# Weighing all four heads of a graph-attention layer's edge messages on one engine instead of two

## The chip, the cores and the metric

The kernel runs on one core of one Trainium2 chip. The metric is the device time of one execution in microseconds (us); a lower time is better. A core has several engines that work side by side and wait for one another through semaphores: TensorE (PE, matmuls; PEld is its weight load), VectorE (DVE), ScalarE (ACT), GpSimd (POOL, which here also issues the gathers) and SyncE (SP, which issues plain transfers).

## The reference, cut to what matters

The program is four graph layers, one after the other, over 6250 nodes and 100000 edges. The change touches the first layer only, a graph attention with four heads of 64 columns:

```python
h = (x @ W).reshape(n, HEADS, C)                 # HEADS = 4, C = 64
e = a_src[src] + a_dst[dst]; e = jnp.where(e >= 0, e, NEG_SLOPE * e)
m = jax.ops.segment_max(e, dst, num_segments=n)
alpha = jnp.exp(e - m[dst])
denom = jax.ops.segment_sum(alpha, dst, num_segments=n)
alpha = alpha / (denom[dst] + 1e-16)
msg = alpha[:, :, None] * h[src]
out = jax.ops.segment_sum(msg, dst, num_segments=n)
```

The product `alpha * h[src]` is what is called weighing below: each gathered row of 256 values is multiplied, head by head, with four weights of its edge.

## The kernel before

The edges are sorted by destination and cut into 832 steps of 128 edges. Four steps are a group, 32 steps (eight groups) are a block, and there are 26 blocks. `gat_edges` (lines 580 to 919) runs them; `ends_apart` (line 95) writes the first and the last round out and loops over the others, two blocks to a round. The work of two blocks overlaps: in one turn, the logits, maxima and weights of block n are computed while block n-1 is weighed and summed, and block n+1 is gathered.

For one group the steps are these. GpSimd gathers four times 128 rows of 260 values from the node table into `e_rows` (line 664). The weights, `exp` of the logit less the maximum, are written once per block by ScalarE into PSUM (line 696) and once more beside the rows (line 698). Then the rows are weighed: VectorE takes heads 0 and 1 of the whole group in one operation (line 804, 128 partitions x 512 values), and ScalarE takes heads 2 and 3 in eight small ones (line 676, 128x64 each, one per step and head). VectorE counts up `weighed`, ScalarE `half_weighed`. TensorE waits for both (lines 722 and 723) and for the one-hot matrix of the group (line 924), and sums each step's rows by destination into one of four PSUM banks (line 727). VectorE adds each sum to the accumulator of its node tile (line 821).

The order of the work is written out by hand, engine by engine. For each group q of a turn VectorE weighs group q, adds the four sums of group q-1, and makes the one-hot matrix of group q+1; at q = 3 to 7 the work of the next block is put in between (logits at line 829, scans at lines 838 and 840, links at lines 846 to 853, tops at lines 860 to 868, arguments at line 900), and from q = 4 on two `spread` operations per q (line 788), whose data SyncE brings (line 650). GpSimd's gathers of group q of block n+1 go into the buffer of block n-1, so they wait until TensorE has summed group q of block n-1 (semaphore `summed`, lines 661 and 662). ScalarE's order in a turn is: weigh groups 0 to 3, copy the gather indices of block n+2 when block n has landed (line 691), weigh groups 4 and 5, `exp` for the rescale (line 694), weigh groups 6 and 7, and the two `exp` of the weights (lines 696 and 698). After the last turn the eight groups of the last block are weighed and summed with nothing beside them.

Of the kernel before, what the change touches and what calls it, by code (L numbers as in the profile page):

```python
# [18 lines left out]
ALU = mybir.AluOpType  # L19
ACT = mybir.ActivationFunctionType  # L20
AX = mybir.AxisListType

P = 128
N = 6250
E = 100000
D = 256
# [5 lines left out]
GROUP = 4  # L32
# [547 lines left out]
def gat_edges(nc, k):  # L580

    H = 4
    SB = P // H
    BLOCKS = STEPS // SB
    GB = SB // GROUP
    ROUNDS = BLOCKS // 2
# [4 lines left out]
    with ExitStack() as ctx:  # L591
        def sb(name, shape, dt=F32):
# [4 lines left out]
        idx = [sb(f"e0_idx{u}", [P, SB], I32) for u in range(2)]  # L597
        rows = [sb(f"e0_rows{u}", [P, SB, W]) for u in range(2)]
# [10 lines left out]
        step_down = sb("e0_step_down", [1, H])  # L609
        shrink = sb("e0_shrink", [1, H])  # L610
# [8 lines left out]
        drow_landed = [sem(f"e0_drow_landed{q}") for q in range(RING)]  # L619
        tables_landed = [sem(f"e0_tables_landed{u}") for u in range(2)]  # L620
        (spread_ready, looked_up, logit_ready, turned, local_ready, ends_ready, links_ready, step_ready, shrink_ready,
         back_ready, arg_ready, weight_ready, weighed, half_weighed, onehot_ready, summed, added, chain, cleared, half_cleared) = (
             sem(f"e0_{n}") for n in (
                 "spread_ready", "looked_up", "logit_ready", "turned", "local_ready", "ends_ready", "links_ready",
                 "step_ready", "shrink_ready", "back_ready", "arg_ready", "weight_ready", "weighed", "half_weighed", "onehot_ready",
                 "summed", "added", "chain", "cleared", "half_cleared"))
        block = ctx.enter_context(nc.Block())
        dloc_rows = k.rows_dloc.rearrange("(o s) l -> o (s l)", o=1)
# [39 lines left out]
        @block.scalar  # L668
        def _(act):
            for u in range(2):  # L670
                act.copy(idx[u][:], k.src_idx[:, u * SB:(u + 1) * SB]).then_inc(idx_ready, 1)
            def weigh(n, u, q):
                for s in range(q * GROUP, (q + 1) * GROUP):
                    for h in range(H // 2, H):
                        at = slice(h * (D // H), (h + 1) * (D // H))
                        ins = act.activation(rows[u][:, s, at], rows[u][:, s, at], ACT.Copy,  # L676
                                             scale=rows[u][:, s, D + h:D + h + 1])
                ins.then_inc(half_weighed, 1)

            for it in ends_apart(act, ROUNDS):  # L680
                for u in range(2):
                    n = it * 2 + u
                    start = isinstance(it, int) and it == 0 and u == 0
                    for q in range(GB):
                        if not start:
                            if q == 0:
                                act.wait_ge(weight_ready, 2 * n)
                            weigh(n - 1, 1 - u, q)
                        if q == 3 and not (isinstance(it, int) and it == ROUNDS - 1):
                            act.wait_ge(gathered[u], (it + 1) * (16 * SB))  # L690
                            act.copy(idx[u][:], k.src_idx[:, bass.ds((n + 2) * SB, SB)]).then_inc(idx_ready, 1)
                        if q == 5:
                            act.wait_ge(step_ready, n + 1)
                            act.activation(shrink[:], step_down[:], ACT.Exp).then_inc(shrink_ready, 1)
                    act.wait_ge(arg_ready, n + 1)
                    act.activation(k.psum[:, WEIGHT, 0:P], logit[:].rearrange("p h s -> p (h s)"), ACT.Exp
                                   ).then_inc(weight_ready, 1)
                    act.activation(by_step(rows[u][:, :, D:D + H]), logit[:], ACT.Exp).then_inc(weight_ready, 1)
            act.wait_ge(weight_ready, 2 * BLOCKS)
            for q in range(GB):  # L700
                weigh(BLOCKS - 1, 1, q)

        @block.tensor
        def _(pe):
            pe.sem_inc(summed, 2 * SB)
            pe.sem_inc(looked_up, 2)

            def look_up(n, q, js):
                g = n * GB + q
                pe.wait_ge(spread_ready, g + 1 + RING)  # L710
                for s in range(GROUP):
                    at = (q * GROUP + s) * 3 * H
                    ins = pe.matmul(k.psum[:, LOOK, at:at + 3 * H], spread[q % 2][:, s * P:(s + 1) * P],
                                    k.att16[:, bass.ds(js[q % 4 * GROUP + s], 1), :, :]
                                    .rearrange("p o h c -> p (o h c)"), start=True, stop=True)
                ins.then_inc(looked_up, 1)

            def block_steps(n, half):
                return load_indices(nc, pe, k.step_j, n * SB + half * 16, 16, NODE_TILES - 1)

            def add_up(n, u, q):
                pe.wait_ge(weighed, n * GB + q + 1)
                pe.wait_ge(half_weighed, n * GB + q + 1)
                pe.wait_ge(onehot_ready, n * GB + q + 1 + 1)
                for s in range(GROUP):
                    pe.wait_ge(added, n * NADD + q * GROUP + s + (3 if q else 1))
                    pe.matmul(k.psum[:, s, 0:W], onehot[q % 2][:, s, :], rows[u][:, q * GROUP + s, :],  # L727
                              start=True, stop=True).then_inc(summed, 1)

            for half in range(2):  # L730
                js = block_steps(0, half)
                for q in range(half * 4, half * 4 + 4):
                    look_up(0, q, js)
            for it in ends_apart(pe, ROUNDS):
                for u in range(2):
                    n = it * 2 + u
                    start = isinstance(it, int) and it == 0 and u == 0
                    end = isinstance(it, int) and it == ROUNDS - 1 and u == 1
                    for q in range(GB):
                        if not start:  # L740
                            add_up(n - 1, 1 - u, q)
                        if q == 3:
                            pe.wait_ge(logit_ready, n + 1)
                            pe.transpose(k.psum[:, TURN, 0:P], logit[:].rearrange("p h s -> p (h s)"), k.ident[:]
                                         ).then_inc(turned, 1)
                        if q == 4:
                            pe.wait_ge(local_ready, n + 1)
                            pe.matmul(k.psum[0:1, TURN, P:2 * P], local[:, P - 1:P], k.ident[:], start=True, stop=True)
                            pe.matmul(k.psum[0:1, TURN, 2 * P:3 * P], local[:, 0:1], k.anti[:], start=True, stop=True
                                      ).then_inc(ends_ready, 1)  # L750
                            pe.transpose(k.psum[:, BACK, 0:P], local[:], k.ident[:])
                        if q == 5:
                            pe.wait_ge(links_ready, n + 1)
                            pe.matmul(k.psum[:, BACK, P:3 * P], k.ones_row[:],
                                      links[:].rearrange("o a h s -> o (a h s)"), start=True, stop=True)
                            pe.wait_ge(shrink_ready, n + 1)
                            pe.matmul(k.psum[:, BACK, 3 * P:3 * P + H], k.ones_row[:], shrink[:], start=True, stop=True
                                      ).then_inc(back_ready, 1)
                        if q >= 4 and not end:
                            if q % 2 == 0:  # L760
                                js = block_steps(n + 1, (q - 4) // 2)
                            for ahead in (2 * (q - 4), 2 * (q - 4) + 1):
                                look_up(n + 1, ahead, js)
            for q in range(GB):
                add_up(BLOCKS - 1, 1, q)

        @block.vector
        def _(dve):
# [29 lines left out]
            def weigh(n, u, q):  # L798
                if q == 0:
                    dve.wait_ge(weight_ready, 2 * n + 2)  # L800
                at = slice(q * GROUP, (q + 1) * GROUP)
                w = k.psum[:, WEIGHT, 0:P].rearrange("p (h s) -> p s h", h=H)[:, at, 0:H // 2]
                half = rows[u][:, at, 0:D // 2].rearrange("p s (h c) -> p s h c", h=H // 2)
                dve.tensor_tensor(half, half, w.unsqueeze(3).to_broadcast([P, GROUP, H // 2, D // H]), ALU.mult
                                  ).then_inc(weighed, 1)

            def rescale(n, j):
# [2016 lines left out]
```

## Time and profile before

| | us |
|---|---|
| median of three runs | 6793.4 |
| lowest and highest | 6783.46 and 6804.74 |
| profiled execution | 6801.05 |
| span of the profiled execution, first to last instruction | 6799.1 |
| VectorE busy over the span | 4607.3 (68%) |
| ScalarE busy over the span | 2723.6 (40%) |
| GpSimd busy over the span | 4049.3 (60%) |
| TensorE busy over the span | 4665.7 (69%) |

All four layers share these totals, and the first layer's edges are one stage from about 250 to 1543 us. The views that are used are: the busy time of each engine in stretches of the span; the groups of instructions by line in a stretch; the timeline of one engine, in which each row has the start, the duration, the engine, the line, what is written from what, a count, and in brackets the idle time before it and what ended it; the view of one line, with its shortest, median and longest duration; and the list of waits. "issue" in brackets means that the profile shows nothing that the engine waited for. A DMA that is named as the releaser by a name of another stage (`n_x<-in_x`) stands for a semaphore that was used again: in this stage GpSimd's gathers wait for TensorE's sums and for the index copy alone.

### The profile page before, as it was taken

The page shows a single profiled execution, that of the slowest core. Times are in us where ns is not written, and L with a number is a line of the kernel's source. Part 1 is how long each engine was busy: PE and PEld are TensorE (multiplying, and loading weights), DVE is VectorE, ACT ScalarE, POOL GpSimd, SP SyncE. Part 2 cuts the span into 40 slices and gives each one's busy share as a digit, 9 for nine tenths or more (in the row PEclk, how much of TensorE's full clock was granted, in tenths as well). Part 3 has the DMA queues.
Part 4 walks back from the last instruction along what each step waited for, and adds up shares of the span by engine and source line. Part 5 has one row for each costly group of instructions (what it writes and reads, how often), then busy time and mean ns, then how long its engine had stood idle before and what let it go on. Part 6 is the DMA issues. An engine that isn't in the chain of part 4 may idle for free. (4 is left out here: it accounts for less than half of the span.)

```text
span 6799.1 us, 102254 instructions
## 1 busy us (share of the span) xinstructions
PE 4665.7 (69%) x18460; PEld 3459.3 (51%) x18461; DVE 4607.3 (68%) x11409; ACT 2723.6 (40%) x8089; POOL 4049.3 (60%) x3687
## 2 busy tenths in 40 slices
PE   7366666660566666787777777775577777777799
PEld 5233433340333343466666666664455555555688
DVE  4366666668445445577777777775589999999554
ACT  0133333345233333342111111112288998899543
POOL 1566666641666666525888888883367777777110
PEclk9576676775677767797777777777788888889899
DMA  6344444434555555414888888886556666666110
GB/s 205 105 108 108 108 109 109 109 78 134 170 176 180 178 176 178 138 65 94 136 135 135 134 135 135 135 129 186 179 163 185 188 189 190 183 189 186 37 32 28
DMA packets 697432, 941.29 MB, mean 138 GB/s; under 512 B 98671, under 2 KB 553935, under 8 KB 697264
## 3 DMA queue, kind: packets, MB, share of 16 engines
q0 software_dynamic: 270896, 581.23, 37.1%
q1 hardware_dynamic: 406928, 338.53, 17.2%
q10 hardware_dynamic: 19440, 19.79, 0.8%
q14 instruction: 124, 1.02, 0.0%
q8 instruction: 44, 0.72, 0.0%
HBM read 756.06 MB, written 183.11 MB: 138 GB/s over the span
## 5 line engine op out<-in xcount | busy, mean ns | idle before, releaser
L1810 POOL DMA_INDIRECT gcn<-c_update,c_target x784 | 1231.7, 1571 | 258.7 <-issue 208.9
L664 POOL DMA_INDIRECT e_rows<-hrow,e_idx x832 | 823.4, 990 | 466.5 <-issue 230.1
L2186 POOL DMA_INDIRECT s_rows<-kv,s_idx x832 | 797.6, 959 | 391.6 <-issue 222.9
L1202 POOL DMA_INDIRECT g_rows<-x,g_idx x784 | 776.5, 990 | 386.9 <-issue 226.9
L727 PE MATMUL psum<-e_rows,e_onehot 128*128 128x265 f32 x1664 | 637.5, 537 | 231.5 <-issue 97.7
L1321 PE MATMUL psum<-g_rows,g_onehot 128*128 x1664 | 614.9, 534 | 222.3 <-ACT g_rows L1225 174.0
L2300 PE MATMUL psum<-queries_sums,s_spread 128*128 x1664 | 540.6, 482 | 248.7 <-issue 123.5
L1283 DVE TENSOR_TENSOR acc<-acc,psum 128x1024 f32 x208 | 253.6, 1219 | 596.5 <-remote 352.4
L1321 PEld LDWEIGHTS psum<-g_rows,g_onehot 128*128 128x128 f32 x1664 | 423.4, 267 | 428.9 <-issue 352.6
L727 PEld LDWEIGHTS psum<-e_rows,e_onehot 128*128 128x128 f32 x1664 | 380.6, 253 | 428.9 <-issue 194.6
L1783 ACT COPY acc<-psum 128x512 f32<-128x512 f32 x208 | 121.8, 586 | 1183.1 <-PE psum L1742 758.7
L1765 PE MATMUL psum<-support,acc 128*128 x1664 | 586.7, 514 | 0.0
L1742 PE MATMUL psum<-acc 128*128 128x128 f32 x1664 | 324.1, 356 | 367.3 <-DVEq L1661 256.7
L2300 PEld LDWEIGHTS psum<-queries_sums,s_spread 128*128 128x128 f32 x1664 | 378.5, 238 | 375.8 <-issue 312.7
L2248 ACT ACTIVATE s_rows<-s_rows 128x32 f32<-128x32 f32 x2496 | 549.3, 306 | 1.7
L821 DVE TENSOR_TENSOR acc<-acc,psum 128x265 f32 x832 | 357.5, 430 | 280.0 <-issue 143.2
L1225 ACT ACTIVATE g_rows<-g_rows (+1 forms) x196 | 207.1, 1056 | 787.1 <-DVE g_rows L1276 644.9
L1742 PEld LDWEIGHTS psum<-acc 128*128 128x128 f32 x1664 | 290.3, 259 | 451.1 <-issue 307.1
L1765 PEld LDWEIGHTS psum<-support,acc 128*128 128x128 f32 x1664 | 413.9, 261 | 72.3 <-issue 0.3
L2315 PE MATMUL psum<-s_rows,s_onehot 128*128 128x264 f32 x1664 | 429.0, 403 | 9.0 <-ACT s_onehot L2240 5.8
L2468 DVE SCALAR_TENSOR_TENSOR queries_sums<-queries_sums,keep,psum 128x264 f32 x832 | 400.3, 481 | 41.8 <-issue 20.5
L676 ACT ACTIVATE e_rows<-e_rows 128x64 f32<-128x64 f32 x1664 | 406.9, 334 | 9.4 <-issue 8.4
(387 smaller groups left out, 9580.1 us busy)
## 6 DMA issues: line engine op xcount, KB each, us to landing
g_attr<-in_edge_attr SPq DMA_DIRECT2D x196, 512.0 KB
acc<-rows_src SPq DMA_DIRECT2D x208, 256.0 KB
e_drow<-rows_dloc SPq DMA_DIRECT2D x208, 128.0 KB
acc<-in_edge_feat SPq DMA_DIRECT2D x832, 32.0 KB
s_drow<-rows_dloc SPq DMA_DIRECT2D x208, 128.0 KB
n_sums<-gcn SPq DMA_DIRECT2D x100, 256.0 KB
e_rows<-hrow,e_idx POOLq DMA_INDIRECT x832
edge_rows<-c_edge_rows SPq DMA_DIRECT2D x208, 64.0 KB
```

The costliest lines, as they stand in the source:

```text
L664: pool.indirect_dma_start(rows[u][:, s, 0:D + H], None, k.hrow, bass.IndirectOffsetOnAxis(ap=idx[u][:, s:s + 1], axis=0)).then_inc(gathere ...
L676: ins = act.activation(rows[u][:, s, at], rows[u][:, s, at], ACT.Copy, scale=rows[u][:, s, D + h:D + h + 1])
L727: pe.matmul(k.psum[:, s, 0:W], onehot[q % 2][:, s, :], rows[u][:, q * GROUP + s, :], start=True, stop=True).then_inc(summed, 1)
L1202: pool.indirect_dma_start(rows[:, s, :], None, k.x1, bass.IndirectOffsetOnAxis(ap=idx[:, s:s + 1], axis=0)).then_inc(gathered[n % ROUND], 16)
L1321: pe.matmul(parts[:, bass.ds(to[st], 1), :].rearrange("p o d -> p (o d)"), onehot[q % 2][:, s, :], rows[:, bass.ds(m[st], 1), :].rearrange ...
L1742: ins = pe.matmul(k.psum[:, b, s * P:(s + 1) * P], onehot[b][:, s, :], same[b][:, s, :], start=True, stop=True)
L1765: ins = pe.matmul(k.psum[:, 2 + 2 * b + s // 2, (s % 2) * D:(s % 2 + 1) * D], mix[b][:, s * P:(s + 1) * P], k.support[:, bass.ds(j[q * GRO ...
L1810: pool.indirect_dma_start(k.gcn[a], bass.IndirectOffsetOnAxis(ap=target[:, at:at + 1], axis=0), update[:, at, :], None, compute_op=ALU.add ...
L2186: pool.indirect_dma_start(rows[at.u][:, st, 0:2 * D], None, k.kv, bass.IndirectOffsetOnAxis(ap=idx[at.u][:, st:st + 1], axis=0)).then_inc( ...
L2248: ins = act.activation(mine, mine, ACT.Copy, scale=rows[at.u][:, s, 2 * D + h:2 * D + h + 1])
L2300: ins = pe.matmul(k.psum[:, LOOK + s // 2, (s % 2) * D:(s % 2 + 1) * D], spread[at.b][:, s * P:(s + 1) * P], k.q[:, bass.ds(j[s], 1), :].r ...
L2315: pe.matmul(k.psum[:, s, 0:W], onehot[at.b][:, s, :], rows[at.u][:, at.q * GROUP + s, D:SLOT], start=True, stop=True).then_inc(summed, 1)
```

## The change

VectorE's weighing of a group goes from heads 0 and 1 to all four heads, still in one operation (128x512 becomes 128x1024, with the weights read from PSUM as before). ScalarE's weighing function, its eight calls per turn and the eight calls after the last turn are gone, as is the semaphore `half_weighed` with TensorE's wait for it. ScalarE's index copy and its `exp` for the rescale keep their order, without the weighings between them.

```diff
         def _(act):
-            def weigh(n, u, q):
-                for s in range(q * GROUP, (q + 1) * GROUP):
-                    for h in range(H // 2, H):
-                        at = slice(h * (D // H), (h + 1) * (D // H))
-                        ins = act.activation(rows[u][:, s, at], rows[u][:, s, at], ACT.Copy,
-                                             scale=rows[u][:, s, D + h:D + h + 1])
-                ins.then_inc(half_weighed, 1)
-
             for it in ends_apart(act, ROUNDS):
                 for u in range(2):
                     n = it * 2 + u
-                    start = isinstance(it, int) and it == 0 and u == 0
-                    for q in range(GB):
-                        if not start:
-                            if q == 0:
-                                act.wait_ge(weight_ready, 2 * n)
-                            weigh(n - 1, 1 - u, q)
-                        if q == 3 and not (isinstance(it, int) and it == ROUNDS - 1):
-                            act.wait_ge(gathered[u], (it + 1) * (16 * SB))
-                            act.copy(idx[u][:], k.src_idx[:, bass.ds((n + 2) * SB, SB)]).then_inc(idx_ready, 1)
-                        if q == 5:
-                            act.wait_ge(step_ready, n + 1)
-                            act.activation(shrink[:], step_down[:], ACT.Exp).then_inc(shrink_ready, 1)
+                    if not (isinstance(it, int) and it == ROUNDS - 1):
+                        act.wait_ge(gathered[u], (it + 1) * (16 * SB))
+                        act.copy(idx[u][:], k.src_idx[:, bass.ds((n + 2) * SB, SB)]).then_inc(idx_ready, 1)
+                    act.wait_ge(step_ready, n + 1)
+                    act.activation(shrink[:], step_down[:], ACT.Exp).then_inc(shrink_ready, 1)
...
-            act.wait_ge(weight_ready, 2 * BLOCKS)
-            for q in range(GB):
-                weigh(BLOCKS - 1, 1, q)
...
             def add_up(n, u, q):
                 pe.wait_ge(weighed, n * GB + q + 1)
-                pe.wait_ge(half_weighed, n * GB + q + 1)
                 pe.wait_ge(onehot_ready, n * GB + q + 1 + 1)
...
                 at = slice(q * GROUP, (q + 1) * GROUP)
-                w = k.psum[:, WEIGHT, 0:P].rearrange("p (h s) -> p s h", h=H)[:, at, 0:H // 2]
-                half = rows[u][:, at, 0:D // 2].rearrange("p s (h c) -> p s h c", h=H // 2)
-                dve.tensor_tensor(half, half, w.unsqueeze(3).to_broadcast([P, GROUP, H // 2, D // H]), ALU.mult
+                w = k.psum[:, WEIGHT, 0:P].rearrange("p (h s) -> p s h", h=H)[:, at, :]
+                part = rows[u][:, at, 0:D].rearrange("p s (h c) -> p s h c", h=H)
+                dve.tensor_tensor(part, part, w.unsqueeze(3).to_broadcast([P, GROUP, H, D // H]), ALU.mult
                                   ).then_inc(weighed, 1)
```

## Rows read from the trace of the kernel before

**Rows 1.** Busy time of each engine in a stretch of the stage (PE, PEld, DVE, ACT, POOL)
```profile
300.00:1400.00 1100.00, 702.73 (x2346) 430.37 (x2345) 698.91 (x1749) 362.73 (x1496) 704.28 (x711) 0.70 0.41 109
```

**Rows 2.** Groups of instructions by line, 300 to 1475 us: busy, mean, idle before
```profile
L664 POOL DMA_INDIRECT e_rows<-hrow,e_idx x758 | 752.2, 992 | 423.0 <-issue 207.1 <-DMA n_x<-in_x 144.2 <-PE psum L727 71.7
...
L804 DVE TENSOR_TENSOR e_rows<-e_rows,psum 128x512 f32<-128x512 f32 x188 | 127.9, 680 | 4.1 <-issue 4.1
```

**Rows 3.** Timeline of GpSimd: gathers at which a block's turn begins
```profile
392.92 1.27 POOL L664 DMA_INDIRECT e_rows<-hrow,e_idx  x1 [2.27 <-PE psum L727]
...
1337.98 1.28 POOL L664 DMA_INDIRECT e_rows<-hrow,e_idx  x1 [2.26 <-PE psum L727]
```

**Rows 4.** Timeline of GpSimd: one block's turn and the begin of the next
```profile
1139.44 1.28 POOL L664 DMA_INDIRECT e_rows<-hrow,e_idx  x1 [2.86 <-PE psum L727]
...
1164.11 0.96 POOL L664 DMA_INDIRECT e_rows<-hrow,e_idx  x1 [0.30 <-issue]
1168.86 0.95 POOL L664 DMA_INDIRECT e_rows<-hrow,e_idx  x1 [3.78 <-DMA n_x<-in_x]
...
1182.20 0.95 POOL L664 DMA_INDIRECT e_rows<-hrow,e_idx  x1 [2.89 <-DMA n_x<-in_x]
...
1188.71 1.27 POOL L664 DMA_INDIRECT e_rows<-hrow,e_idx  x1 [1.78 <-PE psum L727]
```

**Rows 5.** Timeline of VectorE: the weighing of group 5 and an add after it
```profile
1152.24 0.68 DVE L804 TENSOR_TENSOR e_rows<-e_rows,psum 128x512 f32<-128x512 f32 x1
...
1158.72 0.43 DVE L821 TENSOR_TENSOR acc<-acc,psum 128x265 f32 x1 [3.00 <-issue]
```

**Rows 6.** VectorE's register operations of line 818 from 1153 to 1168 us
```profile
L818 DVEq ALU_OP  x4: 16/696/702, 1153.0 to 1160.8; - x4
```

**Rows 7.** Those of line 819 from 1139 to 1151 us
```profile
L819 DVEq ALU_OP  x12: 40/40/40, 1139.5 to 1149.4; - x12
```

**Rows 8.** Timeline of VectorE: weighings of groups 6, 7 and 0, a wait between
```profile
1168.35 0.68 DVE L804 TENSOR_TENSOR e_rows<-e_rows,psum 128x512 f32<-128x512 f32 x1
...
1173.82 0.68 DVE L804 TENSOR_TENSOR e_rows<-e_rows,psum 128x512 f32<-128x512 f32 x1
...
1179.52 0.35 DVE L788 TENSOR_SCALAR e_spread<-e_drow,lane 128x512 bf16<-128x512 bf16 x1 [2.00 <-issue]
...
1183.28 0.68 DVE L804 TENSOR_TENSOR e_rows<-e_rows,psum 128x512 f32<-128x512 f32 x1
```

**Rows 9.** Page, costliest groups: a VectorE operation of 1024 values with PSUM input
```profile
L1283 DVE TENSOR_TENSOR acc<-acc,psum 128x1024 f32 x208 | 253.6, 1219 | 596.5 <-remote 352.4
```

**Rows 10.** Timeline of ScalarE: weighings of groups 0 to 3, a wait of the next turn
```profile
1128.14 7.75 ACT L676 ACTIVATE e_rows<-e_rows 128x64 f32<-128x64 f32 x32
...
1166.64 0.20 ACT L694 ACTIVATE e_shrink<-e_step_down 1x4 f32<-1x4 f32 x1 [24.10 <-issue]
```

**Rows 11.** Timeline of VectorE: the weighing of group 0 in that turn
```profile
1133.81 0.69 DVE L804 TENSOR_TENSOR e_rows<-e_rows,psum 128x512 f32<-128x512 f32 x1 [0.42 <-issue]
```

**Rows 12.** List of waits, 300 to 1500 us: waiter, releaser, us, times, longest
```profile
PE psum L727 <- ACT e_rows L676: 23.8, 11, 4.7
```

**Rows 13.** TensorE's wait for `half_weighed`, 300 to 1475 us: shortest, median, longest ns
```profile
L723 PEldq EVENT_SEMAPHORE  x176: 6/51/51, 334.9 to 1420.8; - x176
```

**Rows 14.** Timeline of TensorE: the eight matmuls that sum group 4
```profile
1148.63 3.12 PE L727 MATMUL psum<-e_rows,e_onehot 128*128 128x265 f32 x8 [0.61 <-DVE acc L821]
```

**Rows 15.** Timeline of VectorE: two weighings of the last block
```profile
1533.30 0.68 DVE L804 TENSOR_TENSOR e_rows<-e_rows,psum 128x512 f32<-128x512 f32 x1
...
1536.77 0.68 DVE L804 TENSOR_TENSOR e_rows<-e_rows,psum 128x512 f32<-128x512 f32 x1
```

**Rows 16.** Timeline of GpSimd: another block's turn, with one more wait in it
```profile
1238.55 1.27 POOL L664 DMA_INDIRECT e_rows<-hrow,e_idx  x1 [2.27 <-PE psum L727]
...
1274.07 0.95 POOL L664 DMA_INDIRECT e_rows<-hrow,e_idx  x1 [1.02 <-issue]
...
1287.97 1.40 POOL L664 DMA_INDIRECT e_rows<-hrow,e_idx  x1 [1.77 <-PE psum L727]
```

More of the change, by code:

```diff
@@ L621, in gat_edges @@
         (spread_ready, looked_up, logit_ready, turned, local_ready, ends_ready, links_ready, step_ready, shrink_ready,
-         back_ready, arg_ready, weight_ready, weighed, half_weighed, onehot_ready, summed, added, chain, cleared, half_cleared) = (
+         back_ready, arg_ready, weight_ready, weighed, onehot_ready, summed, added, chain, cleared, half_cleared) = (
              sem(f"e0_{n}") for n in (
                  "spread_ready", "looked_up", "logit_ready", "turned", "local_ready", "ends_ready", "links_ready",
-                 "step_ready", "shrink_ready", "back_ready", "arg_ready", "weight_ready", "weighed", "half_weighed", "onehot_ready",
+                 "step_ready", "shrink_ready", "back_ready", "arg_ready", "weight_ready", "weighed", "onehot_ready",
                  "summed", "added", "chain", "cleared", "half_cleared"))
```

## Prediction, made before the changed kernel was run

> **What bounds the kernel now.** I read the busy time by stretch first. Between 300 and 1400 us VectorE is busy 699 of 1100 us, GpSimd 704, TensorE 703 and ScalarE 363 [rows 1]: no engine is full, so the stage turns in a ring of waits, and what counts is which waits close it. The groups by line say who waits longest: the gathers, 758 of them, have 423 us of idle time before them, of which 207 us are the usual 0.30 us from one to the next and 216 us (144.2 + 71.7) end with TensorE's sums [rows 2].
>
> The timeline of GpSimd then gives the beat. The turns of 19 blocks lie between 392.92 and 1337.98 us, which makes 49.7 us for a block [rows 3]. In the turn that I take as the pattern, GpSimd begins at 1139.44 us, issues 20 gathers without a break (groups 0 to 4), ends the last at 1165.1, waits 3.78 us for the sum of group 5, issues eight, waits 2.89 us for group 7, issues four, and waits 1.78 us for group 0 of the next block, which it starts at 1188.71 [rows 4]. A gather takes 0.95 us and 0.30 to the next, so 32 of them need about 40.5 us of the 49.3; the rest is waiting.
>
> VectorE's timeline shows why the sums are late. Up to group 5 its operations follow one another without a gap, but after the weighing of group 5 at 1152.24 idle time that ends in "issue" lies before each add, 3.00 us of it before the one at 1158.72 [rows 5]. Its register operations, 40 ns each between 1139 and 1151 us [rows 7], take up to 702 ns between 1153 and 1168 [rows 6]. Such a slow stretch shows in nearly every turn, as I read the timelines. It begins 12 to 15 us after GpSimd has begun its 20 gathers and ends 2 to 3 us after it has stopped (1165.1 to about 1167.8), and a shorter one lies behind the next eight gathers (2.00 us of idle time before 1179.52 [rows 8]). What makes the register operations slow I can't read from the trace, only that it goes with a long unbroken run of gathers.
>
> So a turn has two parts. From 1139.4 to about 1167.8 GpSimd sets the time: VectorE's slow stretch ends when the gathers do, whatever VectorE had to do before it. From 1167.8 to 1188.7, some 21 us, VectorE sets it: it weighs groups 6 (1168.35), 7 (1173.82) and 0 of the next block (1183.28) [rows 8], TensorE sums group 0, and that sum starts GpSimd again.
>
> **The change, part by part.** *Longer weighings.* One of 128x512 takes 680 ns [rows 2]. An addition of 1024 values with one input in PSUM, of the same engine and type, takes 1219 ns [rows 9], and I take it for the new one, since only the number of values differs. That is +0.54 us each, 208 times: +112 us of VectorE's busy time. The bounds are 0.54 us and, if the narrow pattern (64 values per weight) cost per head, twice 680 = 1360 ns, or +0.68 us; I take 0.54.
>
> *Where they lie.* There are 24 turns in which a next block is gathered. In each, the weighings of groups 1 to 5 fall in the part that GpSimd sets; I cost them at nothing, and the cover is the wait for the end of 20 gathers. The sums of groups 1 to 4 stay ahead of the gathers: VectorE needs about 3.3 us for a group (3.47 in the last block [rows 15]), 3.9 after the change, GpSimd 5.0. If that cover is gone, they cost up to 5 x 0.54 = 2.7 us a turn. The weighings of groups 6, 7 and 0 are on the path: 3 x 0.54 = 1.6 us a turn.
>
> *The end.* In the last turn and in the last block after it nothing is gathered, and VectorE goes without a gap, 3.47 us from one weighing to the next [rows 15]. All 16 weighings are on the path there: 16 x 0.54 = 8.6 us.
>
> *ScalarE.* Its 1664 small weighings go. One run of 32 takes 7.75 us [rows 10], so a group takes 1.94 us, over 400 us of work in all. Was any of it on the path? At 1166.64 ScalarE has waited 24.10 us for VectorE's step [rows 10], and it weighs groups 0 to 3 from 1128.14 on, while VectorE comes to them only at 1133.81 [rows 11]. TensorE's waits put down to it are 23.8 us in 11 cases [rows 12], against 158 groups; in those that I looked at, VectorE's weighing ended later than ScalarE's, so I count no gain. If all of it were real, it would be -24 us. The index copy keeps its place, as it waits for the landing of the gathers and not for the weighings; the two `exp` come when VectorE's argument does. The cover that hid ScalarE's weighings is not used by anything else.
>
> *TensorE.* One wait per group goes, 51 ns each [rows 13]. Three groups a turn lie on the path, and 16 at the end: 24 x 3 x 0.05 = 3.6 us and 0.8 us less.
>
> **A rule to weigh.** Gathers beside VectorE's work take 0.95 us mostly, 1.27 to 1.40 us now and then [rows 4, 16], and the mean is 0.99 [rows 2]; nothing in the rows ties the long ones to the weighings. The Trainium skill, in "SBUF — State Buffer", section "SBUF: two separate sides", says that VectorE and GpSimd contend for one pair of ports, which an operation holds to its end, if VectorE runs in a two-port mode or reads two inputs from SBUF. The weighing reads one input from SBUF and one from PSUM, so by that rule it doesn't stop a gather at any length, and the sum stays as it is. Were it otherwise, GpSimd's own part would grow by as much as 8 x 0.54 us a turn, which is the same price as the first rival's.
>
> **The sum.** 24 x 1.6 + 8.6 - 3.6 - 0.8 = 38.9 + 8.6 - 4.4 = 43 us, with 24 x 1.62 = 38.9. The profiled execution had 6801.05 us (its span is 6799.1, the median of the three runs 6793.4, 7.7 us lower); on it the sum gives 6844 us, on the median 6793.4 + 43 = 6836.5 us. The prediction is of the median. About 0.3% (20 us) is what a measurement can tell from no change.
>
> **The rivals.** *Everything is on the path.* If the slow stretch begins at a place in VectorE's program and not at a time after GpSimd's start, it moves back with VectorE and its length stays: then all eight weighings count, 24 x 8 x 0.49 + 7.8 = 102 us, or 6895 us. For it speaks that the stretch begins near group 5 in most turns; against it, that it ends with GpSimd's stop in nearly all.
>
> *A leftover.* Between the forecast and this one: VectorE comes to the slow stretch 1.6 to 2.1 us later, does less in it, and takes up to 2 us of work along to the other side of it. That gives 43 + 48 = 91 us at the most, 6884 us. I count it to the forecast's own range.
>
> *The gathers hide it.* The eight gathers that follow have their own slow stretch, in which VectorE waits 2.00 us before 1179.52 [rows 8], and it ends with them. It can hide weighings 6 and 7. In the turn from 1238.55 to 1287.97 GpSimd waited once more, 1.02 us at 1274.07 [rows 16], and yet that turn took 49.4 us, less than the mean of 49.7. Then only the weighing of group 0 counts: 24 x 0.49 + 7.8 = 20 us, 6813 us; if that is hidden too, 8 us, 6801 us.
>
> *Faster.* The 20 gathers run through because the sum of group 4 is out (its matmuls run from 1148.63 to 1151.75 [rows 14]) just as the slow stretch begins (about 1152 [rows 5]). With VectorE some 2 us later it may come too late. Then GpSimd stops after 16 gathers, 5.0 us earlier, the slow stretch ends 5.0 us earlier, and GpSimd pays with one more wait of about 3.4 us. That is 1.6 us a turn gained, as VectorE and not GpSimd sets the rest: 43 us becomes -24 x 1.6 + 7.8 = -31 us, 6763 us. It decides when the slow stretch begins before group 4 is summed. Against it: a wait more has made no turn clearly shorter.
>
> *It doesn't do what it says.* If the operation took 1360 ns or more, the forecast's sum would be 24 x 3 x 0.68 + 16 x 0.68 - 4.4 = 55 us, 6849 us, or with everything on the path 6928 us.
>
> **How the numbers follow.** Forecast, with its leftover, 0.45 (its own range 6815 to 6884); everything on the path 0.20; the gathers hide it 0.20; faster 0.12; a dearer operation 0.03. The range runs from 6785 to 6908: it takes in the first three, and leaves out the faster case and the dearest one. Of the signs: slower by over 0.3% is the forecast, the first rival, the dearer operation and a quarter of the hidden case, 0.67 with what the forecast may lose; within 0.3% is most of the hidden case and the edges of the forecast and of the faster one, 0.23; faster 0.10.
>
> **What would show it.** Right: line 804 with 1024 values at about 1.22 us; the turns, read as the distance of gathers that end a wait for group 0, at about 51.2 us; 20 gathers in the first run; the weighings of groups 6, 7 and 0 further apart by 0.54 us each; the last block's weighings 4.0 us apart. Wrong: a turn of 53 to 54 us (everything counts), of 49.7 (hidden), or shorter with a first run of 16 gathers (faster). If the register operations are no longer slow, or slow for longer, my reading of the slow stretch as bound to the gathers is what fails.

## The result, and the profile after

The changed kernel takes 6831.5 us (median of six runs, 6820.1 to 6838.5), the kernel before 6792.8 us beside it (six runs): the ratio is 1.0054, with a 95% interval from 1.0041 to 1.0067. That is 37 to 39 us slower; 43 us were forecast. The profiled execution, the slowest of its six, has 6838.5 us against 6801.05, and a span of 6836.6 us. In it the stage's last sum ends 42.7 us later than before (1583.2 against 1540.5 us).

The new operation, in the view of its line (shortest, median and longest duration in ns, then who waited for it in us and times), and below it the gathers and the weighings in the groups by line from 300 to 1475 us, which answer to [rows 2]:

```profile
L785 DVE TENSOR_TENSOR e_rows<-e_rows,psum x208: 1195/1214/1222, 287.5 to 1578.9; 128x1024 f32<-128x1024 f32 x104
...
  PE psum L708: 84.6, 48
```

```profile
L664 POOL DMA_INDIRECT e_rows<-hrow,e_idx x735 | 716.5, 975 | 458.6 <-issue 220.9 <-PE psum L708 177.9 <-remote 59.8
...
L785 DVE TENSOR_TENSOR e_rows<-e_rows,psum 128x1024 f32<-128x1024 f32 x184 | 223.2, 1213 | 14.9 <-issue 14.8
```

It takes 1213 ns instead of 680, so +0.53 us. Over 20 turns the busy time by engine (PE, PEld, DVE, ACT, POOL) is, for before and then for after:

```profile
392.00:1386.00 994.00, 634.90 (x2123) 388.18 (x2121) 630.14 (x1579) 329.62 (x1360) 635.27 (x640) 0.70 0.41 109
```

```profile
394.00:1419.00 1025.00, 654.35 (x2122) 394.62 (x2121) 715.68 (x1580) 21.34 (x81) 623.53 (x640) 0.67 0.40 105
```

VectorE is busy 85.5 us longer in 20 turns (4.3 us a turn), and the 20 turns are 31 us longer (1.6 us a turn). The other 54.5 us came out of VectorE's idle time, which fell from 363.9 to 309.3 us. ScalarE's 308 us of work in them are gone. The granted clock of TensorE (the number before the last two) is 0.67 instead of 0.70.

The beat, from GpSimd's timeline, beside [rows 3]: the turns of 20 blocks lie between these two gathers, 51.25 us each (before, over the same 20 blocks, from 392.92 to 1386.58: 49.68).

```profile
394.44 1.27 POOL L664 DMA_INDIRECT e_rows<-hrow,e_idx  x1 [1.99 <-PE psum L708]
...
1419.42 0.95 POOL L664 DMA_INDIRECT e_rows<-hrow,e_idx  x1 [2.90 <-issue]
```

The turns are no longer alike. Of the 20, ten begin with 20 gathers in a run, as all of the same 20 did before, and last 52.2 us on average; the other ten begin with 16 and last 50.3 us. (Outside these 20, the trace of before has two such turns as well, of 51.2 and 46.6 us.) One of each, the gathers that end a wait (beside [rows 4]); where the profile names no engine of this core as the releaser it writes `remote`:

```profile
446.62 1.27 POOL L664 DMA_INDIRECT e_rows<-hrow,e_idx  x1 [3.00 <-PE psum L708]
478.40 0.95 POOL L664 DMA_INDIRECT e_rows<-hrow,e_idx  x1 [6.56 <-PE psum L708]
485.23 0.95 POOL L664 DMA_INDIRECT e_rows<-hrow,e_idx  x1 [1.63 <-PE psum L708]
490.38 0.95 POOL L664 DMA_INDIRECT e_rows<-hrow,e_idx  x1 [0.44 <-issue]
498.81 0.95 POOL L664 DMA_INDIRECT e_rows<-hrow,e_idx  x1 [3.20 <-PE psum L708]
```

```profile
596.88 0.95 POOL L664 DMA_INDIRECT e_rows<-hrow,e_idx  x1 [2.47 <-PE psum L708]
620.32 0.95 POOL L664 DMA_INDIRECT e_rows<-hrow,e_idx  x1 [3.31 <-remote]
632.59 0.95 POOL L664 DMA_INDIRECT e_rows<-hrow,e_idx  x1 [2.52 <-remote]
647.25 0.95 POOL L664 DMA_INDIRECT e_rows<-hrow,e_idx  x1 [4.88 <-PE psum L708]
```

In the first of them GpSimd waits 6.56 us after 20 gathers, where before it waited 3.78 [rows 4]. These are two different waits, and TensorE's timeline tells them apart. Here are the last matmuls of group 5's sum before (1162.00), of group 5's sum in the first turn (475.45), and all those of group 4's sum in the second turn (608.87):

```profile
1162.00 1.25 PE L727 MATMUL psum<-e_rows,e_onehot 128*128 128x265 f32 x2 [1.54 <-issue]
```

```profile
475.45 2.14 PE L708 MATMUL psum<-e_rows,e_onehot 128*128 128x265 f32 x4 [1.55 <-DVE acc L802]
```

```profile
608.87 2.44 PE L708 MATMUL psum<-e_rows,e_onehot 128*128 128x265 f32 x8 [1.15 <-DVE e_rows L785]
```

A gather that waits for a sum starts 0.8 us after the sum's last matmul. The first turn shows it: the sum ends at 477.59 and the gather starts at 478.40. Before, the sum of group 5 ended at 1163.25, ahead of the end of the twentieth gather (1165.07), and the next gather still started only at 1168.86, 5.6 us after it. So the 3.78 us of [rows 4] aren't the wait for the sum of group 5, as the prediction reads them. They end just after VectorE's slow stretch does (about 1167.8). It is so in all 20 turns of before: the wait is 3.3 to 3.9 us long, whether the sum ended 2.1 or 11.8 us before the gather starts, and in 17 turns the sum was out before GpSimd stopped.

The turns that begin with 16 gathers in the changed kernel have the same wait (sum out at 611.31, gather at 620.32; 2.6 to 9.3 us after the sum in all ten). In its ten turns with 20 gathers the gather starts 0.81 or 0.82 us after the sum: there the sum itself is late. What holds GpSimd in the other case no record shows.

VectorE's timeline of the first turn shows why the sum of group 5 is late, and what became of the late weighings (beside [rows 5] and [rows 8]):

```profile
461.91 1.21 DVE L785 TENSOR_TENSOR e_rows<-e_rows,psum 128x1024 f32<-128x1024 f32 x1
467.97 0.43 DVE L802 TENSOR_TENSOR acc<-acc,psum 128x265 f32 x1 [4.85 <-issue]
472.16 0.43 DVE L802 TENSOR_TENSOR acc<-acc,psum 128x265 f32 x1 [3.77 <-issue]
...
478.91 1.21 DVE L785 TENSOR_TENSOR e_rows<-e_rows,psum 128x1024 f32<-128x1024 f32 x1
...
484.91 1.21 DVE L785 TENSOR_TENSOR e_rows<-e_rows,psum 128x1024 f32<-128x1024 f32 x1
...
492.65 1.22 DVE L785 TENSOR_TENSOR e_rows<-e_rows,psum 128x1024 f32<-128x1024 f32 x1 [0.33 <-issue]
```

Group 5 is weighed 15.3 us after the turn's begin (12.8 before) and group 6 at 32.3 us (28.9 before). From there to the next turn's begin it is 19.9 us, against 20.4 before. In the mean of 20 turns it is 29.05 us before and 30.61 after from the begin to the weighing of group 6, and 20.63 and 20.63 from there to the next begin: all of the growth lies in the part that I had called covered. But this is the mean of two kinds of turns. The ten with 20 gathers have 32.10 and 20.12 us, the ten with 16 have 29.13 and 21.15.

In the end it is 4.00 us from one weighing of the last block to the next, where [rows 15] have 3.47. From the stage's last gather to its last sum it is 65.3 us, against 58.1 before, so the end costs 7.2 us where 8.6 were reckoned:

```profile
1566.93 1.21 DVE L785 TENSOR_TENSOR e_rows<-e_rows,psum 128x1024 f32<-128x1024 f32 x1
1570.93 1.21 DVE L785 TENSOR_TENSOR e_rows<-e_rows,psum 128x1024 f32<-128x1024 f32 x1
```

### The profile page after: what moved, and what is told of

It is laid out like the page before. It is cut to its first block and busy times, and to the rows that moved or that the text cites. A ratio compares the mean times of both kernels' runs of the same rounds, so it can differ in the third digit from the quotient of the medians.

```text
span 6836.6 us, 100360 instructions
## 1 busy us (share of the span) xinstructions
PE 4685.1 (69%) x18460; PEld 3458.6 (51%) x18461; DVE 4725.0 (69%) x11409; ACT 2321.3 (34%) x6425; POOL 4037.1 (59%) x3687
## 5 line engine op out<-in xcount | busy, mean ns | idle before, releaser
L708 PE MATMUL psum<-e_rows,e_onehot 128*128 128x265 f32 x1664 | 670.7, 558 | 337.1 <-issue 128.5
L1302 PE MATMUL psum<-g_rows,g_onehot 128*128 x1664 | 629.8, 544 | 210.7 <-ACT g_rows L1206 172.4
L1264 DVE TENSOR_TENSOR acc<-acc,psum 128x1024 f32 x208 | 253.6, 1219 | 598.0 <-remote 327.8
L1682 DVE SCALAR_TENSOR_TENSOR c_update<-c_update,acc,psum 128x256 f32 x832 | 399.9, 481 | 12.2
```

What stands on the lines that cost most here:

```text
L1302: pe.matmul(parts[:, bass.ds(to[st], 1), :].rearrange("p o d -> p (o d)"), onehot[q % 2][:, s, :], rows[:, bass.ds(m[st], 1), :].rearrange ...
```

## Experiments

Three theories were held against each other: (1) the prediction's, by which the gathers cover the weighings of groups 1 to 5 and groups 6, 7 and 0 are paid; (2) every weighing is paid; (3) the early ones are paid in part, at the slow stretch. The runs met two conditions, which the time of the kernel before, taken beside each of them, tells apart: 6800.5 and 6804.4 us in the one, like the first measurement, and 6333.6 and 6333.2 us in the other. I call them the 6800 us and the 6333 us condition; the expectations below speak of chips with and without slow stretches. That the chip makes the difference isn't shown: the record numbers the chips, and has number 12 for the first group of runs at 6800 us, number 5 for one at 6333 us, and number 3 for one of each. Every ratio is against before in the same group of runs.

### Without gathers

Edit, in both kernels: from block 2 on nothing is gathered, and the waits for landed rows are met by a plain count. The first layer's sums are others, so only the time is read.

```diff
+                        if isinstance(it, int) and it == 0:
...
+                        else:
+                            pool.sem_inc(skipped[u], 1)
```

> The kernel before, with the gathers of blocks 2 to 25 left out (rows of the first two blocks are weighed again and again, so the first layer's sums are others). What is left is the pace of VectorE and TensorE alone. Theory 1: the slow stretches come with the gathers, so no register operation of VectorE takes 0.7 us, and a turn is VectorE's busy time of 31.6 us plus short waits, 33 to 36 us, the stage 330 to 400 us shorter where there were slow stretches. Rival (the slow stretches are VectorE's own, code or registers): they stay, and a turn is 45 us or more on a chip that shows them.

> The changed kernel with the same gathers left out. Theory 1 (without gathers VectorE alone sets the turn, so every weighing counts): 8 x 0.54 = 4.3 us more per turn than the kernel before without gathers, less up to 0.4 us for TensorE's wait; 24 x 4.0 = +96 us and +8 us at the end. Rival (TensorE or ScalarE sets the turn there, and the weighings are hidden): under 2 us more per turn.

Measured, one execution each, in the 6800 us condition (before 6800.5 us): 6488.1 us for before without gathers, 6577.4 us for after without them, so 89 us apart. The logits of two blocks that are 20 turns apart, from VectorE's timeline of each, give a turn of 36.34 and of 39.99 us:

```profile
410.33 0.55 DVE L840 TENSOR_REDUCE e_logit<-psum 128x128 f32<-128x384 f32 x1
...
1137.11 0.55 DVE L840 TENSOR_REDUCE e_logit<-psum 128x128 f32<-128x384 f32 x1
```

```profile
423.16 0.55 DVE L821 TENSOR_REDUCE e_logit<-psum 128x128 f32<-128x384 f32 x1
...
1223.03 0.55 DVE L821 TENSOR_REDUCE e_logit<-psum 128x128 f32<-128x384 f32 x1
```

The register operations before an add (the wait for a sum), shortest, median and longest in ns; the kernel before as it is, then before without gathers:

```profile
L819 DVEq ALU_OP  x704: 5/40/710, 338.3 to 1426.1; - x176
```

```profile
L830 DVEq ALU_OP  x704: 40/40/40, 327.8 to 1123.9; - x176
```

What follows: with the gathers out, VectorE is busy 622 of 727 us in 20 turns before and 706 of 800 after, and 3.65 of the 4.3 us of added work are paid in a turn. With them in, only 1.6 are. So the gathers do hide work of VectorE. And the slow register operations need the gathers: not one of the 704 takes over 40 ns without them, in either kernel, while the changed kernel with gathers had up to 1142 ns in the same group of runs. The sizes were expected a little otherwise: before without gathers became 312 us shorter, not 330 to 400, and 89 us lie between the two where 104 were expected.

### ScalarE's work gone, VectorE's as before

Edit: the changed kernel, but VectorE weighs heads 0 and 1 alone.

```diff
-                w = k.psum[:, WEIGHT, 0:P].rearrange("p (h s) -> p s h", h=H)[:, at, :]
-                part = rows[u][:, at, 0:D].rearrange("p s (h c) -> p s h c", h=H)
+                w = k.psum[:, WEIGHT, 0:P].rearrange("p (h s) -> p s h", h=H)[:, at, 0:H // 2]
+                half = rows[u][:, at, 0:D // 2].rearrange("p s (h c) -> p s h c", h=H // 2)
```

> ScalarE's weighings and TensorE's wait for them are gone, and VectorE weighs heads 0 and 1 alone as before; heads 2 and 3 stay unweighed, so the kernel leaves that part of the computation out. Theory 1 (ScalarE is never on the path): -4 us against before from TensorE's wait alone, turns at 49.6 us, which can't be told from no change. Rival (TensorE's 23.8 us of waits that the profile puts down to ScalarE are real, or ScalarE's work slows others): -24 us or more, turns at 48.7 us.

Measured: 6333.5 us against 6333.6, ratio 1.0001 (0.9992 to 1.0010), in the 6333 us condition. ScalarE's 1664 weighings weren't on the path there. But GpSimd's gathers follow one another without a break in that condition, so hardly anything that is taken from ScalarE could show. In the 6800 us condition, in which the prediction had costed ScalarE, it wasn't run alone.

### The weighings split by group

Edit for the early ones (groups 1 to 5 on VectorE alone, 0, 6 and 7 shared as before); for the late ones the two sets change places (the first lines are VectorE's, the next TensorE's, the last ScalarE's):

```diff
+                heads = H // 2 if q in (0, 6, 7) else H
-                w = k.psum[:, WEIGHT, 0:P].rearrange("p (h s) -> p s h", h=H)[:, at, 0:H // 2]
+                w = k.psum[:, WEIGHT, 0:P].rearrange("p (h s) -> p s h", h=H)[:, at, 0:heads]
...
+                if q in (0, 6, 7):
+                    pe.wait_ge(half_weighed, n * 3 + (0, 6, 7).index(q) + 1)
...
+                            if q in (0, 6, 7):
+                                weigh(n - 1, 1 - u, q)
```

> VectorE weighs all four heads for groups 1 to 5 of each block, ScalarE keeps heads 2 and 3 of groups 0, 6 and 7 alone. Theory 1 (GpSimd's 20 gathers cover the early groups): the turns stay at 49.7 us, only the 10 wide groups of the end cost, 10 x 0.49 = +5 us against before. Theory 2 (every weighing of VectorE counts): 24 x 5 x 0.49 + 5 = +64 us, turns at 52.2 us. Theory 3 (VectorE comes later to the slow stretch and carries up to 2 us of work over it in turns that still have 20 gathers in a run): +20 to +50 us.

> The complement: VectorE weighs all four heads for groups 0, 6 and 7, ScalarE keeps heads 2 and 3 of groups 1 to 5. Theory 1 (the late groups are the ones on the path): 24 x 3 x 0.49 + 6 x 0.49 = +38 us against before, turns at 51.2 us, nearly the whole of the change's cost. Theory 2 (every weighing counts): the same +38 us, but then the early half costs +64 us and the two don't add up to the change's +38 us. Theory 3 (the later slow stretch hides groups 6 and 7): +12 to +15 us, turns at 50.2 us.

Measured, in the 6333 us condition: early 1.0000 (0.9991 to 1.0010), late 0.9989 (0.9980 to 0.9998). None of the theories was tried by it: there were no slow stretches, and GpSimd gathered without a break. So both were run again:

> Groups 1 to 5 wide on VectorE, groups 0, 6 and 7 shared as before; once more, for a chip with slow stretches. Theory 1 (the gathers cover the early groups): +5 us against before, turns at 49.7 us, first runs of 20 gathers. Theory 3 (VectorE comes to the slow stretch some 2 us later; where the sum of group 4 then comes too late the first run ends at 16 gathers and the turn is 2 us shorter than one with 20): first runs mixed, turns at 49.7 to 51 us, 0 to +30 us. Theory 2 (all count): +64 us. On a chip without slow stretches, all give what was measured there, 0 to +5 us.

> Groups 0, 6 and 7 wide on VectorE, groups 1 to 5 shared as before; once more, for a chip with slow stretches. Theory 1: +38 us against before, turns at 51.2 us, first runs of 20 gathers, since the sum of group 4 is no later than before. If instead the eight gathers' slow stretch hides groups 6 and 7: +12 to +15 us, turns at 50.2 us. If the early groups make the change's cost, this kernel is at 0 to +10 us. On a chip without slow stretches: -9 to +5 us.

Measured: again in the 6333 us condition, early 1.0002 (0.9993 to 1.0011), late 0.9987 (0.9978 to 0.9996). The early ones alone were run a third time:

> Groups 1 to 5 wide, 0, 6 and 7 shared, for the third time, as both runs so far fell on a chip without slow stretches (there: 0 to +3 us). On a chip with them: theory 1 as predicted before the change was run (the 20 gathers cover groups 1 to 5, the cost is in groups 6, 7 and 0) gives +5 us, turns at 49.7 us, 29.0 us from the first gather of a turn to the weighing of group 6. The theory that the changed kernel's trace suggests (the part before group 6 grew from 29.0 to 30.6 us, the part after it stayed at 20.6 us, so the early groups make the cost) gives +30 to +42 us, turns at 51 us, first runs of 16 and of 20 gathers, 30.6 us up to the weighing of group 6.

Measured, in the 6800 us condition: 6819.7 us against 6804.4, ratio 1.0025 (1.0015 to 1.0035), +15 to +17 us. The turn is 50.02 us over 20 turns:

```profile
394.13 0.95 POOL L664 DMA_INDIRECT e_rows<-hrow,e_idx  x1 [2.70 <-DMA n_x<-in_x]
...
1394.51 1.28 POOL L664 DMA_INDIRECT e_rows<-hrow,e_idx  x1 [0.78 <-issue]
```

Fifteen of the 20 turns begin with a run of 16 gathers and last 49.1 us, four with 20 and last 53.2 us, one with four. Up to the weighing of group 6 it is 29.7 us, after it 20.3. Both numbers that were expected are missed: theory 1's +5 us is too little, the +30 to +42 us of the theory formed from the changed kernel's trace too much. The medians put the early groups at something under half of the cost, with their share of the end (10 x 0.53 = 5 us) in it; the rest, 14 to 23 us, is by subtraction the late groups'. That the two parts simply add up isn't shown, as the late groups weren't run alone in this condition. The turns themselves don't bear the subtraction out: those with 16 gathers last 49.1 us here and 50.3 in the changed kernel's first trace (49.9 in its second, below), those with 20 last 53.2 us here and 52.2 (51.8) there.

### The changed kernel again

> The changed kernel once more, beside before on the chip that this call gets. In the four runs so far before took 6333.6 us and not 6793, the turns were 41.0 to 41.4 us, all 32 gathers stood in one unbroken run and no register operation of VectorE was slow. If the chip is again such a one: theory (GpSimd's 32 gathers alone set the turn, 32 x 1.29 = 41.2 us, and VectorE has some 5 us a turn to spare) gives only the end, +8 us against before. If it is one with slow stretches: +37 to +43 us as first measured, turns at 51.2 us. Rival (VectorE's 0.54 us count on every chip): +100 us on either.

Measured, in the 6800 us condition: 6830.9 us against 6800.5, ratio 1.0054 (1.0038 to 1.0069). The ratio of the first result is there again. The profiled execution is the fastest of its six, 6818.9 us. Its turn is 50.25 us, with 14 of 20 turns beginning with 16 gathers and four with 20, and the stage's last sum ends 22.9 us later than in the trace of before, where it was 42.7 us in the first trace. So the mix changes from one execution to the next, and with it the length of the stage.

> The changed kernel on the same chip as the three above, as their measure. On a chip with slow stretches: +37 us against before, turns between 50.2 and 51.3 us with first runs of 16 and of 20 gathers. On a chip without them: theory (GpSimd's gathers alone set the turn) gives the end alone, +8 us; rival (VectorE's work counts) +100 us.

Measured, in the 6333 us condition: 6328.0 us against 6333.2, ratio 0.9987 (0.9978 to 0.9996). It is not slower there at all, by the interval even faster by a trifle, where +8 us were expected. The turn is 41.09 us, no gather of it waits longer than the usual 0.3 us, and no register operation is slow:

```profile
353.58 0.96 POOL L664 DMA_INDIRECT e_rows<-hrow,e_idx  x1 [0.30 <-issue]
...
1175.33 0.95 POOL L664 DMA_INDIRECT e_rows<-hrow,e_idx  x1 [0.31 <-issue]
```

```profile
L800 DVEq ALU_OP  x704: 40/40/40, 303.7 to 1202.3; - x176
```

GpSimd's 32 gathers at 1.28 us are the turn. VectorE's turn of 40 us, as it was without gathers, fits into it with 1 us to spare.

### The late groups wholly on ScalarE

Edit: ScalarE weighs all four heads of groups 0, 6 and 7 as soon as the weights are there, VectorE all four of groups 1 to 5 (first lines ScalarE's, last ones VectorE's).

```diff
+                        for q in (0, 6, 7):
+                            weigh(n - 1, 1 - u, q)
...
+                if q in (0, 6, 7):
+                    return
```

> ScalarE weighs all four heads of groups 0, 6 and 7 (48 small operations a block, right after the weights are there), VectorE all four heads of groups 1 to 5. Theory 1 (late groups on the path, early groups covered): VectorE's 0.60 us falls away three times a turn, 24 x 3 x 0.60 = -43 us, and at the end 6 x 0.60 gained and 10 x 0.54 lost, +2 us: -41 us against before, turns at 47.9 us. Theory 2 (every weighing of VectorE counts alike): -43 + 24 x 5 x 0.54 + 2 = +24 us. Theory 3 (early groups cost about 2 us a turn through the slow stretch): about +5 us.

> ScalarE weighs groups 0, 6 and 7 whole, VectorE groups 1 to 5 whole; once more, for a chip with slow stretches. Theory 1: 24 x 3 x 0.60 = -43 us in the turns and +2 us at the end, -41 us against before, turns at 47.9 us. If the early groups' 0.54 us are paid at the slow stretch: -10 to +5 us. On a chip without slow stretches: -11 us as measured there.

Measured, both times in the 6333 us condition: 0.9985 (0.9976 to 0.9994) and 0.9983 (0.9974 to 0.9992), some 11 us faster than before. It beats before there, and can't be told from the changed kernel (0.9987). In the 6800 us condition, where it was meant to gain 41 us, it wasn't run, and whether it is faster there stays open.

## Why the prediction was right, and where it wasn't

**The price of one weighing** was right: 1213 ns where 1219 were taken, +0.53 us, no dearer for its narrow pattern.

**The end** was right within 1.4 us: 4.00 us between weighings, and 7.2 us from the last gather to the last sum where 16 x 0.54 = 8.6 us were reckoned. **TensorE's shorter wait**, 4.4 us in the sum, is shown by no run: where ScalarE's work and this wait alone were taken out, 4 us less were expected and none measured, in the 6333 us condition.

**ScalarE costed at nothing** was tried only in the 6333 us condition, with 1.0001 when its work alone was taken out. Whether the 23.8 us of waits that the profile puts down to it [rows 12] are real in the 6800 us condition stays open (and the groups that they are set against are 188 by the count of [rows 2], not 158).

**"The gathers cover groups 1 to 5"** is the step that failed, in the turns with 20 gathers. The wait for the end of the 20 gathers did cover VectorE's lateness before, since the sum of group 5 had slack: in the turn of [rows 4] it ended 23.8 us after the begin and its gather started at 29.4. The prediction took GpSimd's stop for a wait for this sum, so it did not see the slack, nor how much of it there was. In the changed kernel's turn VectorE comes to the weighing of group 5 2.5 us later and has the four adds behind it (those of group 4's sums) in the slow stretch, with 4.85 us of idle time before the first. TensorE needs these adds for the sum of group 5, and that now ends 31.0 us after the begin, 7.2 us later. Of these, 4.8 us were slack and 2.4 us are paid. In all ten turns with 20 gathers the sum ends at 29.4 to 31.0 us, against 17.7 to 27.4 before, and they last 52.2 us on average, against 49.7. This is the leftover to which the prediction gave the range only.

**"Groups 6, 7 and 0 are paid"** was wrong in its balance. Group 6 to 7 did take 0.53 us more (5.47 before, 6.00 after; 0.44 us in the mean of 20 turns), and so did the stretch from group 0 to the next begin (0.49 us in the mean). But from group 7 to group 0 it was 9.46 us and is 7.74 in the turn shown, 9.25 and 8.31 in the mean: VectorE's waits for the `spread` rows and its idle time in the second slow stretch shrank. Line 788 had 111.2 us of idle time before its operations from 300 us to the end of the gathers, and its answer in the changed kernel (300 to 1510 us) has 28.2. By the timelines of the 20 turns, 1.6 us a turn of this drop lie between groups 7 and 0, and the larger part, 2.4 us net, ahead of the weighing of group 6:

```profile
L788 DVE TENSOR_SCALAR e_spread<-e_drow,lane 128x512 bf16<-128x512 bf16 x190 | 63.3, 364 | 111.2 <-DMA rows_src<-acc 73.0 <-issue 28.2 <-PE psum L713 6.4
```

```profile
L769 DVE TENSOR_SCALAR e_spread<-e_drow,lane 128x512 bf16<-128x512 bf16 x190 | 63.1, 368 | 28.2 <-DMA rows_src<-acc 16.8 <-issue 7.6 <-PE psum L695 1.1
```

That is akin to the rival "the gathers hide it", at work in the later part of the turn.

**The rival "faster"** is there too, with the sign that it named and without its gain. In half of the turns the first run ended at 16 gathers. The sum of group 4 ended 14.3 to 20.8 us after the begin in these, 13.2 to 14.8 in the other half and 11.6 to 14.3 before, which fits the rival's condition that the sum comes after the slow stretch has begun. But GpSimd's stop isn't the plain wait for it: in 7 of the 10 the sum was out before the sixteenth gather had ended. These turns are 1.9 us shorter than those with 20 (50.3 against 52.2 us) and still 0.6 us longer than before, where the rival had them 1.6 us shorter than before.

**The size was luck in part.** Two kinds of turns, +2.5 and +0.6 us, mixed to a mean of 1.57 us, which happens to lie at the forecast's 1.6. In the second trace of the changed kernel the same code gave +0.57 us a turn. The place was wrong, and the early-groups experiment shows it: +15 to +17 us where the forecast's steps give +5.

**A rival that nobody tried** is TensorE's clock. From 300 us to the end of the gathers the matmuls of the sums take 542 ns in the mean before and 565 after, at a granted clock of 0.70 and 0.67 over the 20 turns (0.69 in the second trace of the changed kernel). That is 0.2 us for the eight matmuls of a sum; how much of the 1.57 us it makes isn't shown.

**The rule that was weighed** held: with a VectorE operation nearly twice as long the gathers did not get longer, their mean went from 992 ns [rows 2] to 975. That agrees with the rule of the Trainium skill's "SBUF — State Buffer", section "SBUF: two separate sides".

**Everything on the path** fell: without gathers 3.65 us a turn are paid, with them 1.6. (The 6928 us that the prediction gives it with the dearer operation don't come out of its terms, which make about 6924; nothing hangs on it.)

**The slow stretch as bound to the gathers** held, but it is half of what it takes: the gathers, and the 6800 us condition. What that condition is stays open.

## What to carry to other kernels

When two engines pace each other in turns, ask of a covered stretch not only what ends it but what else has to be ready at that moment, and how long it has been ready. Compare the end of the work that is waited for with the end of the wait: here a gather that really waited for a sum started 0.8 us after it, and one that started 5.6 us after it waited for something else. The difference is slack, and the work moved into the cover used it up and came out behind it as a late sum. Work that is put on a pacing engine can be paid in a different part of the turn than the one it was put in, and the sum may still agree, so split the turn into parts in the trace after, and compare part by part. A gain or loss of half a per cent that hangs on waits may turn with the condition that the kernel meets: 1.0054 in one, 0.9987 in the other. So measure both kernels side by side, and more than one trace of each.

## What the runs showed of the hardware that was not expected

The kernel before took 6333 us in one condition and 6800 us in the other. Some 220 us of it lie ahead of the last sum of this stage (at 1540.5 us in the trace of before, at 1311 to 1322 us in the eight traces of other kernels from the 6333 us condition); the rest lies in the later stages and wasn't looked into. In this stage the difference that the traces show is in the register operations of VectorE: in the 6333 us condition the 704 of the add's wait take 40 ns each, in the 6800 us condition up to 710 ns (before) and 1397 ns (after), and all take 40 ns again when the gathers are left out:

```profile
L800 DVEq ALU_OP  x704: 2/40/1397, 340.1 to 1463.0; - x176
```

SyncE, which brings the `spread` rows, has them too (before, 300 to 1475 us):

```profile
L650 SPq FUSED_REGOPS  x172: 5/37/1383, 307.4 to 1368.0; - x172
```

From 300 to 1200 us of the same trace no register operation of ScalarE or GpSimd and only one of TensorE takes over 300 ns. Yet GpSimd, with the sum that it needs already out, goes on only after the slow stretch has ended (1163.25 to 1168.86 us in the turn of [rows 4]). The changed kernel's turn was 41.1 us in the one condition and 51.3 us in the other. Such register operations aren't counted as busy, so the page shows them as idle time that ends in "issue".
